# A graph kernel: bias rows by TensorE, a second table dropped, and the softmax steps of two convolutions re-laid

## The reference, cut to what matters

```
# layer 0: message passing
msg = leaky_relu([x[src], x[dst], edge_weight] @ W_edge + b_edge)   # slope 0.01
out = leaky_relu([x, segment_sum(msg, dst)] @ W_node + b_node)
# layer 1: two transformer convolutions, 8 heads of 16 channels
alpha = sum(q[dst] * k[src]) / 4          # per edge and head
a     = exp(alpha - segment_max(alpha)[dst]);  a = a / segment_sum(a)[dst]
out   = segment_sum(v[src] * a) + x @ sw + sb;  relu between the two
```

## Time and profile before

| | us |
|---|---|
| median of 3 runs | 3101.77 |
| the profiled execution | 3101.67 |
| its span | 3099.9 |
| PE busy | 2460.4 (79%) |
| DVE busy | 2586.2 (83%) |
| ACT busy | 1926.8 (62%) |
| POOL busy | 1987.3 (64%) |

### The profile page before, as it was taken

How to read it: one execution, slowest core, us unless ns; L and a number is a source line. 1 busy time by engine, 2 the same in 40 slices (tenths; PEclk the granted TensorE clock), 3 DMA queues, 4 the chain that set the end, 5 groups by cost and what they waited for, 6 DMA issues and landing times. The chain is left out here.

```text
span 3099.9 us, 46510 instructions
## 1 busy us (share of the span) xinstructions
PE 2460.4 (79%) x14327; PEld 1739.5 (56%) x14327; DVE 2586.2 (83%) x3231; ACT 1926.8 (62%) x3501; POOL 1987.3 (64%) x1891
## 2 busy tenths in 40 slices
PE   7899999959999996888888589999999961445620
PEld 3466666637777764565666356677777751223410
DVE  6689999969999996999999646898999885999940
ACT  0067677646666665988889557777777733455520
POOL 4477777714334326777777377788778416777776
PEclk9999999979999998999999899999999975657765
DMA  7456767656777765777777436799989777985311
GB/s 210 117 172 217 227 214 225 219 177 194 217 215 214 213 197 175 238 235 229 230 230 233 137 120 170 196 241 220 218 206 245 183 190 246 293 283 159 96 52 39
DMA packets 495871, 611.80 MB, mean 197 GB/s; under 512 B 67257, under 2 KB 285827, under 8 KB 495500
## 3 DMA queue, kind: packets, MB, share of 16 engines
q1 hardware_dynamic: 433814, 495.64, 53.2%
q0 software_dynamic: 56480, 111.88, 13.9%
q10 hardware_dynamic: 5334, 1.32, 0.2%
HBM read 391.94 MB, written 220.55 MB: 198 GB/s over the span
## 5 line engine op out<-in xcount | busy, mean ns | idle before, releaser
L781 POOL DMA_INDIRECT c_xs<-table_x,src_row x196 | 187.4, 956 | 264.5 <-PE c_psT L923 213.0
L1336 POOL DMA_INDIRECT g_xd_xs<-table_x,dst_row x196 | 226.4, 1155 | 122.6 <-issue 57.7
L771 POOL DMA_INDIRECT c_xs<-table_h,src_row x196 | 220.5, 1125 | 116.9 <-issue 78.8
L503 POOL DMA_INDIRECT xs<-in_x,src_i x196 | 227.0, 1158 | 86.2 <-issue 55.5
L488 POOL DMA_INDIRECT xd<-in_x,dst_i x196 | 217.3, 1109 | 94.8 <-issue 48.5
L1893 POOL DMA_INDIRECT out<-f_rows,end_i x196 | 197.4, 1007 | 67.3 <-issue 62.1
L1886 POOL DMA_INDIRECT f_rows<-table_x,src_row x196 | 190.8, 973 | 70.9 <-issue 59.4
L1336 POOL DMA_INDIRECT g_xd_xs<-table_x,src_row x196 | 196.3, 1001 | 59.8 <-issue 59.8
L1430 PEld LDWEIGHTS g_psP<-w_center,g_turns 128*128 128x128 f32 x1568 | 188.3, 194 | 69.4 <-ACT g_turns L1588 41.2
L1937 PE MATMUL f_psT<-w_ident,f_rows 128*128 128x128 f32 x196 | 47.6, 388 | 223.0 <-DVE f_rows L2030 223.0
L771 POOL DMA_INDIRECT c_xd<-table_h,dst_row x196 | 186.1, 949 | 59.7 <-issue 59.7
(11 more groups left out here) (345 smaller groups left out, 8350.2 us busy)
## 6 DMA issues: line engine op xcount, KB each, us to landing
g_share<-shares SPq DMA_DIRECT2D x196, 192.0 KB
xn<-in_x SPq DMA_DIRECT2D x49, 512.0 KB
table_x<-xo SPq DMA_DIRECT2D x49, 512.0 KB
table_x1b<-xb SPq DMA_DIRECT2D x49, 512.0 KB, 4.9
c_xn<-table_x SPq DMA_DIRECT2D x49, 512.0 KB
table_h<-c_xo SPq DMA_DIRECT2D x49, 512.0 KB
c_xn<-table_h SPq DMA_DIRECT2D x49, 512.0 KB
c_x1r<-table_x1b SPq DMA_DIRECT2D x49, 512.0 KB
```

Source lines behind the costliest of these rows:

```text
L503: pool.indirect_dma_start(out=quarters(h.xs0[:, s, :])[j], out_offset=None, in_=io["x0"], in_offset=edge_index(h.src_i, n, j)).then_inc(h. ...
L771: pool.indirect_dma_start(out=quarters(rows[:, s, :])[j], out_offset=None, in_=table, in_offset=edge_index(columns, now.n, j)).then_inc(la ...
L781: pool.indirect_dma_start(out=quarters(xs[:, s, :])[j], out_offset=None, in_=table, in_offset=edge_index(h.src_row, now.n, j)).then_inc(sr ...
L1336: pool.indirect_dma_start(out=quarters(xd_xs[:, s, k, :])[j], out_offset=None, in_=table, in_offset=edge_index(columns, n, j)).then_inc(la ...
```

## The change

Setup: the centred bias row `s_b1c` is split into three bf16 parts that add up to it; row k of the small tile `bias3` (3 x 512) holds part k four times over. `ones3` is 3 x 128 ones. The weight of the edge weights is loaded as a column.

```diff
+            bias_left, parts_sum = h.s_b1c, ew1[:, 0:P]
+            for k in range(3):
+                link(nc.vector.tensor_copy(bias_part[:, :], bias_left[:, :]))
+                if k < 2:
+                    link(nc.vector.tensor_tensor(h.s_b1c[:, :], h.s_b1c[:, :], bias_part[:, :], ALU.subtract))
+                place_in = h.w["ident"][:, k:k + 1]
+                if k == 0:
+                    link(nc.vector.tensor_scalar(parts_sum, bias_part[:, :], place_in, None, ALU.mult))
+                else:
+                    link(nc.vector.scalar_tensor_tensor(out=parts_sum, in0=bias_part[:, :], scalar=place_in,
+                                                        in1=parts_sum, op0=ALU.mult, op1=ALU.add))
+            link(nc.vector.tensor_copy(by_row(h.bias3[:, :]), parts_sum[0:3, :].rearrange(
+                "p (o f) -> p o f", o=1).to_broadcast([3, 4, P])))
```

```diff
-                    nc.tensor.matmul(psZ[:, 0, :], h.w_edge_row[:, :], erow[:, now.slot, :],
...
+                if now:
+                    dve.wait_ge(z_ready, now.n + 1)
+                    dve.wait_ge(ew_landed[now.slot], 16 * (now.half + 1))
+                    wait(dve, z01_ready, now.n)
+                    nc.vector.scalar_tensor_tensor(out=z[:, :], in0=ew[:, now.slot, :], scalar=h.w_edge_col[:, :],
+                                                   in1=psZ[:, 0, :], op0=ALU.mult, op1=ALU.add).then_inc(z_added, 1)
-                        nc.vector.tensor_tensor(wide(xb[:, g3.slot, :, :]), wide(xo[:, g3.slot, 0:2, :]),
-                                                h.s_b1c[:, :].rearrange("p (o f) -> p o f", o=1).to_broadcast([P, 8, P]),
-                                                ALU.add).then_inc(xb_ready, 1)
...
-                    sp.dma_start(node_rows(io["x1b"], g.n), xb[:, g.slot, :, :]).then_inc(xb_stored[g.slot], 16)
```

```diff
-                    nc.vector.tensor_tensor_scan(m[:, s, 1:TILE + 1], h.far[:, here], psA[:, :], m[:, s, 0:1],
-                                                 ALU.add, ALU.max).then_inc(m_ready, 1)
+                    nc.vector.tensor_tensor(m[:, s, 0:1], carry[:, :], h.far[:, bass.ds(last.n * TILE, 1)], ALU.add)
+                    dve.wait_ge(first_ready, last.n + 1)
+                    nc.vector.tensor_tensor_scan(m[:, s, 1:TILE], psA[:, 0:TILE - 1], h.far[:, here], m[:, s, 0:1],
+                                                 ALU.max, ALU.add).then_inc(m_ready, 1)
-                    nc.vector.tensor_tensor(drop[:, :], m[:, s, 0:TILE], m[:, s, 1:TILE + 1],
-                                            ALU.subtract).then_inc(drop_ready, 1)
-                    nc.vector.tensor_tensor(u[:, :], psA[:, :], m[:, s, 1:TILE + 1], ALU.subtract).then_inc(u_ready, 1)
-                    nc.vector.scalar_tensor_tensor(out=dropm[:, :], in0=drop[:, :], scalar=0.0, in1=h.far[:, here],
-                                                   op0=ALU.min, op1=ALU.add).then_inc(dropm_ready, 1)
-                    nc.vector.tensor_copy(m[:, 1 - s, 0:1], m[:, s, TILE:TILE + 1]).then_inc(carry_ready, 1)
+                    nc.vector.tensor_tensor(drop[:, :], m[:, s, :], psA[:, :], ALU.subtract).then_inc(drop_ready, 1)
+                    nc.vector.tensor_tensor(carry[:, :], m[:, s, TILE - 1:TILE], psA[:, TILE - 1:TILE],
+                                            ALU.max).then_inc(carry_ready, 1)
+                    dve.wait_ge(drop_ready, last.n + 1)
+                    nc.vector.tensor_scalar(u[:, :], drop[:, :], 0.0, None, ALU.max).then_inc(u_ready, 1)
+                    nc.vector.tensor_scalar(dropm[:, :], drop[:, :], 0.0, None, ALU.min).then_inc(dropm_ready, 1)
```

The second convolution, beside that. `own_rows` on PE begins with the bias:

```diff
+                if layer:
+                    nc.tensor.matmul(psE[k][:, :], h.ones3[:, :], h.bias3[:, :], start=True, stop=False)
+                for j, (o, x) in enumerate(zip(quarters(psE[k]), quarters(xnT[:, now.slot, k, :]))):
+                    ins = nc.tensor.matmul(o, x, w_own[:, :], start=not layer, stop=not layer or j == 3)
```

More of the change, by code:

```diff
@@ L673, in step @@
                 if now:
-                    act.wait_ge(z_ready, now.n + 1)
+                    act.wait_ge(z_added, now.n + 1)
                     wait(act, msg_ready, now.n)
-                    nc.scalar.activation(z01[:, :], psZ[:, 0, :], ACT.Identity, bias=h.x01b_edge[:, :],
+                    nc.scalar.activation(z01[:, :], z[:, :], ACT.Identity, bias=h.x01b_edge[:, :],
                                          scale=0.01).then_inc(z01_ready, 1)
@@ L866, in step @@
             def step(t):
-                now, last, (g, a, b) = t.tile(0), t.tile(1), t.group(2)
+                now, last = t.tile(0), t.tile(1)
                 soon = t.tile(-1)
@@ L991, in step @@
             def step(t):
-                now, last = t.tile(0), t.tile(1)
+                now, last, soon = t.tile(0), t.tile(1), t.tile(-1)
                 if now:
                     s = now.slot
-                    turn(0, now, xs[:, s, :], src_landed[s], 64 * (now.half + 1))
-                    turn(1, now, xd[:, s, :], dst_landed[s], 64 * (now.half + 1))
+                    if now.n == 0:
+                        turn_edge_rows(now)
                     pe.wait_ge(turned_sb, 4 * now.n + 2)
@@ L1079, in step @@
             def step(t):
-                now, last, (g, a, b) = t.tile(0), t.tile(1), t.group(1)
+                now, last, (g, a, b), (old, a2, b2) = t.tile(0), t.tile(1), t.group(1), t.group(2)
                 if now:
@@ L1089, in step @@
                         nc.scalar.activation(dst, psT[k][:, :], ACT.Copy).then_inc(turned_sb, 1)
+                if old and a2 == 0:
+                    scale_rows(t, old, a2, b2, 0, 4)
+                if last:
+                    act.wait_ge(u_ready, last.n + 1)
+                    wait(act, pv_ready, last.n)
+                    wait(act, den_ready, last.n)
+                    nc.scalar.activation(p[:, :], u[:, :], ACT.Exp, scale=-1.0).then_inc(p_ready, 1)
+                    act.wait_ge(dropm_ready, last.n + 1)
+                    wait(act, num_ready, last.n)
+                    nc.scalar.activation(c[:, :], dropm[:, :], ACT.Exp).then_inc(c_ready, 1)
+                if now:
+                    keep_q(now)
                 if g:
@@ L1215, in step @@
                                                  ALU.mult, ALU.add).then_inc(den_ready, 1)
+                if layer and g:
+                    norm_sum(nc, dve, g, a, b, sq, var, sq_ready, var_ready, rstd_ready)
+                if last:
                     dve.wait_ge(pv_ready, last.n + 1)
```

128 lines of the change are left out of this document (58 added, 70 removed).

## The result

The changed kernel takes 3171.61 us (median of 4 runs, 3169.46 to 3175.08), the kernel before, on the same chip, 3100.78 (3098.66 to 3106.87): a ratio of 1.0227, 95% interval 1.0211 to 1.0243. It is 71 us slower where I forecast 23 faster.

What follows compares the result with a forecast made beforehand. PE was taken to pace layer0, DVE's work the second convolution, DMA waits to hold the first. Terms +3.2 - 1.0 - 15.0 - 2.5 - 0.5 - 10.1 + 1.5 = -24.4 against 3101.67 gave 3077.3, stated as 3078; range 3046 to 3096.

Steps and rivals of the forecast that it cites:

- First layer: layer0: a loop through L642, y, lr, z, tT, L589 sets 10.12 us a step in place of 10.44, -15.0 us.
- the sum: Whole kernel: all terms together give -24.4 us against the profiled 3101.67, so 3077.3; stated as 3078, chance 0.41.
- Setup, tails: Setup's bias split +3.2, layer0's head -1.0 and end -2.5, the second convolution's last groups +1.5 us.
- The first convolution's -3.3: First convolution: it waits for DMA, so less DVE work gains only -0.5 us at its end, bounds 0 and -10.
- What bounds the second convolution: Second convolution: DVE's work, 10.97 us of an 11.34 us step, paces; the new step is 11.13, -10.1 us.
- The failed step of the sum: Second convolution: ACT begins p at 2.73 us after the first column, right behind u, in a step of 11.13.
- The bias products: Second convolution, PE: two bf16 products of 3 rows by 512 columns a tile, 0.43 us each, covered by some 0.13 us.
- The rival that ended on the slow side: Second convolution: bias products at 0.86 us each delay alike, step 11.86, +25 us, 3113 in all; chance 0.09.
- The constant operations: Convolutions' softmax, DVE: u and dropm with a constant take 0.48 us each, 0.40 start to start; bound 0.68.
- First column: Convolutions' softmax, DVE: a new one-column operation, 0.15 us and a wait for itself, 0.19 in all.
- The port pair: Second convolution: u waits some 0.35 us on average for a gather, step 11.48, +7 us, 3094; chance 0.05.
- GpSimd: Second convolution: POOL's 8 gathers a tile at 1.25 us take 10.0 of 11.1 us.

Runs made afterwards that it cites:

- three places: The changed kernel with three places in place of two for xdT in the second convolution: 3081.11 us, ratio 0.9933 to the kernel before.
- scalings first: The changed kernel with ACT's four scalings put between the xsT and xdT copies, in front of the xdT copy: 3111.54 us, ratio 1.0037.
- bias ahead: The changed kernel with PE's first bias product issued ahead of its wait for ACT's copy of the node rows (xnT): 3129.73 us, ratio 1.0089.
- the version with three edits: The changed kernel with three xdT places, the bias product ahead of PE's wait for xnT, and DVE's sum of squares behind num: 3051.10 us, ratio 0.9845.
- z's new place: The version with three edits, plus in layer0 DVE's z moved behind tT of the node rows: 3102.86 us, ratio 1.0010.
- the run with q twice: The changed kernel with the second convolution's q product issued twice into the same bank on PE: 3146.44 us, ratio 1.0158.

## Why the prediction was wrong

- **First layer: right, with its mechanism.** Regular step 10.12 us as worked out, DVE's wait 0.29 for y, PE waiting for tT in every step; -15.5 against -15.0. That DVE's own work was just below the loop holds too (10.12 less 0.29). What the sum had no term for is GpSimd, as told at the end of this list.
- **Setup, tails: right in size** (table above). The first convolution's -3.3 can't be read: in kernels with its code it ran from 447.4 to 454.2 us, and with the code of before from 450.9 to 454.3.
- **What bounds the second convolution, wrong.** I wrote "DVE's work is 10.97 us a step, and it paces", from one wait of 0.37 us. DVE had no other wait, but that wait was where a loop closed. With 0.3 us less work outside this loop DVE merely waited 0.71, at 11.35 a step.
- **The failed step of the sum:** that ACT would be free to begin p as soon as u is there, 2.73 us after the first column. It rests on "ACT's list is 10.3 us long (11.35 less the 1.04 it waits for turned rows)": I counted ACT's waits and took the one for turned rows as the only one. The copy into xdT has another, for its place, ended by the edge products. Before, the turns stood behind the edge products on PE, so whoever had waited for the turns had waited for the place, and the squares stood right behind the copies. The new order on ACT put four scalings, p, c and q between the copy, which the edge products release, and the squares. So p started 4.22 us after the first column (1408.05 to 1412.27), 1.49 later than in the sum, and the step came to 12.64 where 11.13 was forecast, 1.51 more.
- **What goes with it:** "Turning the next edge rows before edge_products costs nothing: those wait for agg" holds for PE: with the old order nothing came back (3173.71). But it looked only at what the edge products wait for, and not at who waits for them. Once the place is free the regular step is 11.12, with a wait of 0.38 against 0.40.
- **The bias products:** taken at 0.43 us each, they follow at 0.32. The rival that ended on the slow side named them as the cause at 0.86 each; that is refuted. They did lie in the loop: leaving both out makes the step 0.33 us shorter.
- **The constant operations:** 0.43 us and 0.34 start to start, where 0.48 and 0.40 were taken. First column 0.18 (0.19). All these are nearly right, and were worth nothing where the stage waits.
- **The clock:** I had no term for it. The stretches at the lower clock cost another 26 of the 88.5 us; the loop's 1.29 us a step cost the rest.
- **The port pair:** u didn't wait for whole gathers. With three places for xdT it took 0.43 us in 48 of 49 steps. In the changed kernel it took 0.43 in 37 of 49 steps, and longer in the 12 in which a gather had begun 0.6 us before it: 0.63 in the first step and 0.57 in the 11 others. That is 0.14 to 0.20 us in a quarter of the steps, where the rival had 0.35 on the mean of all.
- **GpSimd:** the sum had "POOL's gathers are 8 a tile at 1.25 us, 10.0 of 11.1" for the second convolution and nothing for layer0. 1.25 is the distance behind a gather that nothing lengthens. On the mean it is 1.40 in the second convolution with three places, 11.2 us a tile, and 1.44 in layer0 of the changed kernel, 10.4 us a tile in steps of 10.12. In layer0 it costs nothing until the rows gathered ahead run out: in the profiles of three experiments (three places, scalings first, bias ahead) the last step of the layer takes 15.3 to 15.4 us, and PE waits 3.9 to 4.2 us in it for destination rows.

## What to carry to other kernels

When work is moved ahead of something on one engine, look for every wait that was met only because of the old order: take each buffer that the moved work fills, its number of places, and who frees a place. List the waits of each queue by their code, not by the rows of the trace, where a wait that is always met doesn't show. And before a stage is called bound by an engine with one short wait in it, follow that wait around: if it comes back to the same instruction, work that is taken from the engine outside of that loop buys nothing. And where a queue of gathers is never idle, compare its mean distance, not its shortest, with the step.

## What the hardware showed that was not expected

**DVE lengthens a gather of GpSimd's.** A gather takes 0.94 us as a rule, but 2.02 or about 1.2 in some places, at the same place in each step. Gathers and DVE operations in layer0 of the version with three edits:

```profile
387.81 1.22 POOL L517 DMA_INDIRECT xs<-in_x,src_i  x1 [0.31 <-issue]
393.10 2.02 POOL L502 DMA_INDIRECT xd<-in_x,dst_i  x1 [0.30 <-issue]
395.42 0.94 POOL L502 DMA_INDIRECT xd<-in_x,dst_i  x1 [0.30 <-issue]
...
386.99 1.22 DVE L728 TENSOR_TENSOR tT<-lr,nodeT 128x1024 f32<-128x1024 f32 x1
392.54 1.76 DVE L760 TENSOR_TENSOR xo<-cen,rstd 128x1536 f32<-128x1536 f32 x1
394.59 1.82 DVE L717 SCALAR_TENSOR_TENSOR lr<-psY,cols,y 128x1536 f32<-128x1536 f32 x1 [0.29 <-ACT y L703]
```

The gather of 393.10 starts inside xo, which ends at 394.30, and ends 0.82 us after that; the one of 387.81 starts inside tT (ends 388.21) and ends 0.82 after it. The one of 395.42 lies in lr, which reads PSUM, and takes its 0.94. So it goes for all of them: of the 43 gathers of this layer that were inside xo 0.1 us after their start 42 took 2.0 us and one, which met xo's last 0.46 us, 1.28; and of 46 inside lr none was long. While an operation with two inputs in SBUF runs (tT, xo, the scan), a gather that starts ends 0.75 to 0.83 us behind it, or after its 0.94 if that is later; operations with an input in PSUM and the sum of squares, which has one input, lengthen none. z's new place shifted DVE's steps against GpSimd's, and gathers fell under the scan as well:

```profile
406.11 1.89 POOL L517 DMA_INDIRECT xs<-in_x,src_i  x1 [0.30 <-issue]
405.96 1.28 DVE L743 TENSOR_TENSOR_SCAN red<-cont,red,msg 128x512 f32<-128x512 uint8 x1
```

All 45 that fell there took 1.88 us on the mean. In the version without this edit as many gathers meet the scan, but 0.2 us before its end, and take 0.95. The Trainium skill ("SBUF — State Buffer", section "SBUF: two separate sides") has a rule: an operation of VectorE with two inputs in SBUF and a GpSimd operation that reads SBUF lock the shared pair of ports against each other for a whole instruction. These traces agree with it in which operations lengthen a gather, if a gather counts as one that reads SBUF. In the other direction no wait of DVE for a whole gather is seen, only the 0.14 to 0.20 us of u above. That the lock itself is the cause was not tested, only that the long gathers made the rows late.

**PE's waits have a price beyond themselves.** See the run with q twice: 0.86 us more work for PE in each step, in its waits, and 22 to 25 us less in all.

**A bf16 product of 3 rows by 512 columns** is followed by the next product 0.32 us later (1415.89 to 1416.21 us), where each of the two instructions of an f32 product of 128 rows by 512 columns takes 0.43.
